# The summing of scan states into PSUM in quarter tiles of the TensorE array

## The reference, cut to what matters

```python
u, z = split(x @ in_w.T)
u = silu(causal_conv(u) + conv_b)
dt, Bm, Cm = ...            # from u @ xproj_w.T
dA  = exp(dt[..., None] * A)
dBu = (dt * u)[..., None] * Bm[:, :, None, :]
h_t = dA_t * h_(t-1) + dBu_t       # 16 states per channel
y_t = sum over the 16 states of h_t * C_t, plus u_t * D
out = (y * silu(z)) @ out_w.T
```

## Time and profile before

| | |
|---|---|
| time, median of three runs | 3839.55 us |
| the profiled execution: its own time | 3839.99 us |
| its span, first to last instruction | 3838.2 us |
| PE busy in the span | 3341.7 us (87%) |
| PEld, DVE, ACT, POOL busy | 2161.3, 1745.0, 1256.6, 707.7 us |
| mean granted TensorE clock | 0.927 of full speed |
| scan stage of L1_attn, in the span | about us 2211 to 2481 |
| scan stage of L2_attn, in the span | about us 3046 to 3120 |

### The profile page before, as it was taken

The page is one execution under the profiler, slowest core; times in us unless marked ns, Lnnn a source line. Parts: engine busy times, 40 slices in busy tenths (PEclk is TensorE's granted clock), DMA queues, the critical chain, the costliest instruction groups (busy, mean ns, idle before and its releaser), DMA issues. The chain is left out here.

```text
span 3838.2 us, 42957 instructions
## 1 busy us (share of the span) xinstructions
PE 3341.7 (87%) x17208; PEld 2161.3 (56%) x17208; DVE 1745.0 (45%) x3610; ACT 1256.6 (33%) x1940; POOL 707.7 (18%) x338
## 2 busy tenths in 40 slices
PE   6999999999999977788888699889885789978865
PEld 3666666666666655455454366644442456667744
DVE  5555545455454343455555455534331330045544
ACT  3444444444444421244444454222211322211111
POOL 3423234232332200000000055400000120023300
PEclk9999999999999987899898899999987889989977
DMA  3000000000000001300000011111108222132100
GB/s 118 1 21 1 21 1 21 21 1 21 1 21 1 1 4 51 109 18 35 18 18 1 13 31 34 71 65 55 55 30 279 60 85 88 44 131 103 52 11 28
DMA packets 63493, 166.29 MB, mean 43 GB/s; under 512 B 3513, under 2 KB 44625, under 8 KB 60369
## 3 DMA queue, kind: packets, MB, share of 16 engines
q1 hardware_dynamic: 63312, 163.80, 12.3%
HBM read 162.64 MB, written 0.62 MB: 43 GB/s over the span
## 5 line engine op out<-in xcount | busy, mean ns | idle before, releaser
L1304 PE MATMUL L_xattn_bank<-L_xattn_keys_tok,L_xattn_probsT 128*128 128x256 f32 (+2 forms) x1792 | 409.8, 383 | 0.6 <-DVE L_xattn_probsT L991 0.6
L1084 POOL TENSOR_TENSOR L_xattn_k_normed<-L_xattn_k_normed,L_xattn_k_square 128x833 f32<-128x833 f32 (+1 forms) x128 | 248.5, 1959 | 871.4 <-ACT L_xattn_k_square L1155 871.4
L1256 PE MATMUL L_xattn_wide<-L_xattn_keys_feat,weights_a 128*128 128x512 f32 (+2 forms) x1024 | 383.0, 518 | 0.9 <-DVE L_xattn_keys_feat L956 0.9
L1304 PEld LDWEIGHTS L_xattn_bank<-L_xattn_keys_tok,L_xattn_probsT 128*128 128x128 f32 (+2 forms) x1792 | 335.1, 190 | 71.7 <-issue 21.2
L1256 PEld LDWEIGHTS L_xattn_wide<-L_xattn_keys_feat,weights_a 128*128 128x128 f32 x1024 | 185.3, 189 | 165.4 <-issue 140.5
L2810 PE MATMUL L_ffn_bank<-L_ffn_expert_w,L_ffn_hidden 128*128 128x256 f32 x928 | 227.1, 408 | 48.7 <-DVE L_ffn_hidden L2674 36.3
L961 DVE COPY L_xattn_k_normed<-L_xattn_wide 128x833 f32<-128x833 f32 (+1 forms) x128 | 131.4, 1027 | 259.6 <-PE L_xattn_wide L1256 259.6
L2224 DVE TENSOR_TENSOR_SCAN L_attn_state<-L_attn_decay,L_attn_banks 128x1024 f32<-128x1024 f32 x80 | 182.8, 2286 | 138.6 <-PE L_attn_banks L2430 138.6
L2810 PEld LDWEIGHTS L_ffn_bank<-L_ffn_expert_w,L_ffn_hidden 128*128 128x128 f32 x928 | 188.6, 206 | 97.9 <-DVE L_ffn_hidden L2674 38.7
L2332 POOL TENSOR_TENSOR L_attn_state<-L_attn_state,L_attn_C_rows 128x1024 f32<-128x1024 f32 x80 | 188.0, 2351 | 140.2 <-DVE L_attn_state L2224 140.2
L1263 PE MATMUL L_xattn_wide<-L_xattn_k_square,const 128*128 128x512 f32 (+2 forms) x512 | 206.6, 526 | 6.3 <-ACT L_xattn_k_square L1148 6.3
(11 more groups left out here) (429 smaller groups left out, 5303.0 us busy)
## 6 DMA issues: line engine op xcount, KB each, us to landing
L_xattn_ctx_feat<-in_ctx_feat SPq DMA_DIRECT2D x24, 1601.0 KB, 10.0
L_ffn_expert_w<-in_x_L_ffn SPq DMA_DIRECT2D x9, 2568.0 KB, 9.2
L_ffn_expert_w<-in_x_L_ffn SPq DMA_DIRECT2D x8, 2052.0 KB, 7.8
L_xattn_keys_tok<-in_ctx_tok SPq DMA_DIRECT2D x8, 1536.0 KB
L_attn_C_rows<-L_attn_c_rows SPq DMA_DIRECT2D x48, 256.0 KB, 3.1
L_xattn_ctx_tok<-in_ctx_tok SPq DMA_DIRECT2D x8, 1536.0 KB
L_xattn_ctx_tok_and_one<-in_ctx_tok SPq DMA_DIRECT2D x8, 1536.0 KB
weights_a<-in_w_L_xattn SPq DMA_DIRECT2D x1, 4737.0 KB, 16.3
```

Source lines behind the costliest of these rows:

```text
L1084: nc.gpsimd.tensor_tensor(kn[:, s % 2, a:a + n], kn[:, s % 2, a:a + n], sq[:, a:a + n], ALU.mult).then_inc(kn_ready, 1)
L1256: last = nc.tensor.matmul(wide[:, 2 * h + c, 0:n], wk[:, k, p * P:(p + 1) * P], xnT[:, k, a:a + n], start=(k == 0), stop=(k == KT - 1))
L1304: last = nc.tensor.matmul(bS[:, 0:D], pT[0:r, t, :], xn[b % 2][0:r, t, :], start=(t == 0), stop=(t == TILES - 1))
```

## The change

add_state and start_y no longer use the whole array with 128 rows and 128 columns. Each of their matmuls is cut into quarters of 64 rows x 64 columns. The row half r takes channels 64 r to 64 r + 63 of the group j from the state, and the column half j puts the result in partitions 64 j to 64 j + 63 of bank 2q + r. So a piece has four matmuls of 512 columns in place of two, and no two of the four share both halves of the array. The stationary operand is a half of `fold` in place of `ident`, and for start_y a 64-column diagonal in D_diagonal, which is half as large.

y's channels then lie in another order in PSUM. The host packs the z columns of in_w and the rows of out_w in that order, so that no instruction is added for it.

```diff
--- before.py
+++ after.py
@@ -2062,7 +2062,7 @@
         duT = [sb(f"dt_u_tok_{d}", [P, NT, MT * P]) for d in range(ND)]
         dbc = [sb(f"dbc_{d}", [KD, N]) for d in range(ND)]
         bt = [sb(f"B_tok_{d}", [P, NT, NSTATE]) for d in range(ND)]
-        Dd = sb("D_diagonal", [P, ND, MT, P])
+        Dd = sb("D_diagonal", [P, ND, MT, S])
         A = sb("A", [P, ND, MT, NSTATE])
         dA = sb("decay", [P, RING, 2, 2, NT, S])
         h = sb("state", [P, RING, 2, 2, NT, S])
@@ -2316,8 +2316,8 @@
                 pool.wait_ge(w_ready[0], w_ready[1])
                 for d, pre in enumerate(turns):
                     c = at[pre + "D"]
-                    last = nc.gpsimd.tensor_tensor(Dd[:, d, :, :], L.ident.unsqueeze(1).broadcast_to([P, MT, P]),
-                                                   w[:, c:c + MT].unsqueeze(2).broadcast_to([P, MT, P]), ALU.mult)
+                    last = nc.gpsimd.tensor_tensor(Dd[:, d, :, :], L.fold.unsqueeze(1).broadcast_to([P, MT, S]),
+                                                   w[:, c:c + MT].unsqueeze(2).broadcast_to([P, MT, S]), ALU.mult)
                 last.then_inc(D_ready, 1)
                 for d in range(ND):
                     pool.wait_ge(du_ready, (d + 1) * PC)
@@ -2438,14 +2438,19 @@
                         pe.wait_ge(yz_ready, (d - 1) * PC + q + 1)
                     for j in range(2):
                         m = 2 * q + j
-                        nc.tensor.matmul(banks[:, m, :], Dd[:, d, m, :], u[d][:, m, :], start=True, stop=True)
+                        for r in range(2):
+                            nc.tensor.matmul(banks[j * S:(j + 1) * S, 2 * q + r, :], Dd[r * S:(r + 1) * S, d, m, :],
+                                             u[d][r * S:(r + 1) * S, m, :], start=True, stop=True)
 
                 def add_state(p):
                     pe.wait_ge(hC_ready, p + 1)
                     for j in range(2):
-                        y = banks[:, 2 * (p % PC) + j, :].rearrange("p (t r s) -> p r t s", r=2, s=S)
-                        last = nc.tensor.matmul(y, L.ident, h[:, p % RING, :, j, :, :],
-                                                start=False, stop=True, skip_group_check=True)
+                        for r in range(2):
+                            y = banks[j * S:(j + 1) * S, 2 * (p % PC) + r, :]
+                            last = nc.tensor.matmul(y.rearrange("p (t r s) -> p r t s", r=2, s=S),
+                                                    L.fold[r * S:(r + 1) * S, :],
+                                                    h[r * S:(r + 1) * S, p % RING, :, j, :, :],
+                                                    start=False, stop=True, skip_group_check=True)
                     last.then_inc(y_added, 1)
 
                 def project_out(d, t):
@@ -2985,6 +2990,14 @@
     return k
 
 
+def quarter_order(DI):
+    return np.arange(DI).reshape(DI // 256, 2, 2, 64).transpose(0, 2, 1, 3).reshape(-1)
+
+
+def z_in_quarters(w, DI):
+    return np.concatenate([w[:, :DI], w[:, DI:][:, quarter_order(DI)]], 1)
+
+
 def pack_l1_attn():
     k = Pack()
     for n in ("ln_g", "ln_b"):
@@ -2992,11 +3005,11 @@
     DI, R, MT = 512, 96, 4
     for pre in ("f_", "b_"):
         g = lambda i, n, pre=pre: i["L1_attn_" + pre + n]
-        k.add(pre + "in_w", KT * 2 * DI, lambda i, g=g: _rows(g(i, "in_w").T))
+        k.add(pre + "in_w", KT * 2 * DI, lambda i, g=g: _rows(z_in_quarters(g(i, "in_w").T, DI)))
         k.add(pre + "xproj", MT * R, lambda i, g=g: _rows(g(i, "xproj_w").T))
         k.add(pre + "dt_w", DI, lambda i, g=g: np.concatenate(
             [_pad(np.ascontiguousarray(g(i, "dt_w").T))[:R], g(i, "dt_b").reshape(1, DI), np.zeros((P - R - 1, DI), np.float32)]))
-        k.add(pre + "out_w", MT * D, lambda i, g=g: _rows(g(i, "out_w").T))
+        k.add(pre + "out_w", MT * D, lambda i, g=g: _rows(g(i, "out_w").T[quarter_order(DI)]))
         k.add(pre + "conv_w", MT * NCONV, lambda i, g=g: _rows(g(i, "conv_w")))
         for n in ("conv_b", "D"):
             k.add(pre + n, MT, lambda i, g=g, n=n: _col(g(i, n)))
@@ -3012,12 +3025,12 @@
     k = Pack()
     g = lambda i, n: i["L2_attn_" + n]
     DI, R, MT = 256, 33, 2
-    k.add("in_w", KT * 2 * DI, lambda i: _rows(g(i, "in_proj_w").T))
+    k.add("in_w", KT * 2 * DI, lambda i: _rows(z_in_quarters(g(i, "in_proj_w").T, DI)))
     k.add("xproj", MT * R, lambda i: _rows(g(i, "x_proj_w").T))
 
     k.add("dt_w", DI, lambda i: np.where(np.arange(P)[:, None] == 32, 1.0, 0.0).astype(np.float32)
           * np.ones((1, DI), np.float32))
-    k.add("out_w", MT * D, lambda i: _rows(g(i, "out_proj_w").T))
+    k.add("out_w", MT * D, lambda i: _rows(g(i, "out_proj_w").T[quarter_order(DI)]))
     k.add("conv_w", MT * NCONV, lambda i: _rows(g(i, "conv_w")))
     k.add("conv_b", MT, lambda i: _col(g(i, "conv_b")))
     k.add("D", MT, lambda i: _col(g(i, "D_param")))
```

## The result

| | before | after |
|---|---|---|
| median | 3839.38 us (6 runs, 3837.29 to 3847.06) | 3809.55 us (6 runs, 3806.95 to 3817.59) |
| the profiled execution: its own time, its span | 3839.99, 3838.2 us | 3807.82, 3806.1 us |
| mean granted TensorE clock | 0.927 | 0.916 |

What follows compares the result with a forecast made beforehand. TensorE was taken to bound both scan loops, at 3.84 us a piece, to become 2.95. Savings of 59.1 us in L1_attn and 13.5 in L2_attn sum to 72.6; 3839.99 - 72.6 gives 3767 us, range 3754 to 3785.

Steps and rivals of the forecast that it cites:

- What bounds the kernel: Both scan loops: TensorE is busy throughout, 3.84 us a piece; what is taken from it comes off, down to about 2.4.
- Four quarters at once: add_state: four quarters run side by side, so eight instructions take two turns, 1.02 us in place of 1.91.
- two at a time: Rival, add_state: only two quarters run together, four turns as before, time 3840 within 2 us; 5 in 100.
- partial overlap: Rival, add_state: quarters overlap only in part, three turns, 1.45 us an add, 37 us less, 3803; 5 in 100.
- blocking in program order: Rival, add_state: a quarter's second instruction blocks the next quarter, five turns, 2.29 us an add, about 3870; 4 in 100.
- The costs of the changes of tiling: Both ends of add_state: 0.09 us before state_input and as much before the add, left as they are.
- the lower end of the range: 3754 us, for the case that tiling-change costs vanish: 0.18 us less a piece, 14 us in 80 (3753).
- Nothing else comes last: Loops at 2.95 us a piece: scan and multiplication end 4.91 us after state_input, 1.0 us to spare before the add.
- The sum for L1_attn: L1_attn: 54.3 us from 61 adds, 1.4 in the tail, 1.7 at each of two start_y; together 59.1 less.
- The sum for L2_attn: L2_attn: 11.6 us from 13 loop adds, 0.89 from the last, 1.0 at the start; together 13.5 less.
- The clock rival: Rival, new loop: TensorE at 1.2 GHz makes it slower than before; 1 in 100, as the loop is never idle.

Runs made afterwards that it cites:

- extra work spread: Changed kernel with as many quarter matmuls again in L2_attn's pieces from 2 on, in the middle of state_input instead of behind the add: 3839.91 us.

## Why the prediction was wrong

**What bounds the kernel: right.** TensorE bounded both loops, and what was taken from it came off in L1_attn one to one.

**Four quarters at once: right.** The step that no row showed, both directions cut and two row tiles accumulating, came out at 1.02 us an add, the forecast value. The rivals of two at a time, of partial overlap and of blocking in program order are out. The costs of the changes of tiling stayed, since 1.02 and 1.94 us include them; so the lower end of the range was not used. This agrees with the Trainium skill (TensorEngine Tiling, Key Properties), by which a change of mode drains the engine.

**Nothing else comes last: right.** DVE's wait of 0.66 us is the forecast one, and POOL ends a wait of PE only at the start and at the end of the loop. In the tail of L1_attn the kernel after starts its add of piece 62 at 2402.70, 2.00 us after piece 61's at 2400.70, released by POOL, where 2.0 was forecast:

```profile
2400.70 1.09 PE L2450 MATMUL L_attn_banks<-L_attn_state,const 64*64 64x512 f32 x8
2402.70 1.09 PE L2450 MATMUL L_attn_banks<-L_attn_state,const 64*64 64x512 f32 x8 [0.91 <-POOL L_attn_state L2332]
```

**The sum for L1_attn: right**, 58.8 us against 59.1.

**The sum for L2_attn: the step that failed.** It priced 13 adds at 0.89 us of the full clock, and it said of the start that the state_input that moves forward "falls partly in the slow clock, and I take 1.0". Both take for granted that the clock rises where it rose before. But the clock rose at 3052.4 in the fourth turn of start_y, and the change leaves two of them. The loop then ran all its pieces at 5.52 us: 2.57 us a piece over the forecast 2.95, for about 15 pieces 38 us. That is the difference between -13.5 and +24.4.

With the clock up in the loop the sum is nearly met, and a smaller cost shows that it had at nothing: the end of the layer. In the run with start_y done twice, with four turns as before, it is 3043.20 - 2989.43 = 53.8 us from start_y to project_out; before it was 3114.72 - 3049.34 = 65.4. That is 11.6 less, where the sum has 12.5 for the adds. But PE's waits between the last, shorter adds are followed by a fall of the clock at 3040.4, and project_out takes 5.71 us in place of 3.73. Timeline of PE and busy time, run with start_y twice, then PE in the kernel before:

```profile
2989.43 3.51 PE L2442 MATMUL L_attn_banks<-L_attn_u,L_attn_D_diagonal 64*64 64x512 f32 x16
3043.20 5.71 PE L2460 MATMUL L_attn_banks<-weights_b,L_attn_z_gate 128*128 128x256 f32 x16 [1.33 <-DVE L_attn_z_gate L2216]
...
3037.00:3040.40 3.40, 1.37 (x12) 0.41 (x16) 0.58 (x1) 0.00 (x0) 2.46 (x2) 1.00 0.00 0
3040.40:3043.80 3.40, 2.07 (x10) 0.52 (x3) 1.22 (x1) 0.00 (x0) 0.00 (x0) 0.50 0.00 0
...
3114.72 3.73 PE L2455 MATMUL L_attn_banks<-weights_b,L_attn_z_gate 128*128 128x256 f32 x16 [1.32 <-DVE L_attn_z_gate L2216]
```

**The clock rival: the right mechanism, wrongly excluded.** It had 1 in 100, with the reason that the new loop is never idle (it also took the whole kernel to be slower, where one layer was). Idle time is what goes before a fall, and L1_attn's loop indeed never fell. I asked of the loop whether it would lose the clock and never whether it would get it. The rows for that question were there: start_y begins at 0.50 in both layers, and the clock rises while it streams. The Trainium skill (TensorE: Matmul & The Clock Gate, the table of goals in "Why this matters for your kernels") asks that TensorE be kept busy without gaps to have its full clock. Measured here, 191.1 us of gapless work at 0.50 go against this as a rule by busy time alone.

## What to carry to other kernels

When an edit makes dense TensorE work shorter, look not only at the loop it is in but at where the clock rises before it, what the engine did up to that rise, and whether the edit leaves that in place. Each stage that is entered at 1.2 GHz has to be priced at both clocks. Busy shares don't show such a loss, as PE reads 100% at either clock: read the granted clock of every stage beside its length. If a stage hangs at the low clock, putting dense pieces of work that are there anyway next to each other may be enough (35 us here for one moved call), and matmuls of no use in a wait ahead of it may be worth more than they cost.

## What the runs showed of the hardware

- Four 64x64 tiles, fed fp32 and accumulating in two banks, run at once: eight instructions of 512 columns take 1.02 us to the start of the next group, where four on the whole array took 1.91.
- With one program, the loop of the changed kernel has two lasting speeds, 2.95 us a piece at 2.4 GHz and 5.52 at 1.2. It held the full clock for all of L1_attn's loop (5.5 us a piece would have been over 350 us), and the low one for 191 us (L1_attn with its start taken apart) and through L2_attn's loop. What it had at its entry decided, as long as no four turns came to stand together in it.
- At every rise of the clock from start_y to the last add in these two layers, four turns of 512 columns stood together, on the whole array or in quarters alike. The rise came 2.1 us (3098.78 to 3100.9, extra work spread) to 4.4 us (2998.00 to 3002.4, adds doubled) after the first of them began, so in the third or fourth turn or right behind them; whether all four are needed isn't shown. Two and two with small matmuls between them, in each of 14 pieces, never did it.
- Such turns aren't the only work ahead of a rise. Before L1_attn's scan, in the kernel before, PE ran 16 instructions of 128 columns (L2389, 3.67 us from 2205.71), and the clock was at 1.00 from 2209.3. Which other small matmuls do this, and why state_input's don't, wasn't tried.
